# Every matmul of the mixture's up and down products is issued as two of 256 tokens with the same weights

## The reference

```python
ctx = causal_ema(x, tau_ctx)
wg = sigmoid([x, ctx] @ Wg.T + bg); gated = x * wg
h1 = gelu(x @ Wn1.T + bn1); mod = 0.5 + sigmoid(h1 @ Wn2.T + bn2)
traces = [causal_ema(gated * mod[d], tau[d]) for d in range(8)]
temporal = sum(traces * softmax(blend))
gate = sigmoid(temporal @ Wtemp.T + btemp); soma = gelu(x @ Wsoma.T + bsoma)
x = x + layernorm((soma * gate) @ Wout.T) * gamma + beta
```

```python
s0, s1, s2 = [relu(x @ share_wi[i]) @ share_wo[i] for i in range(3)]
expert_out = wa * relu(x @ expert_wi[t]) @ expert_wo[t] + wb * relu(x @ expert_wi[t + 1]) @ expert_wo[t + 1]
g = softmax(relu([expert_out[:, 0], s0[:, 0], s1[:, 0], s2[:, 0]] @ gate_w1) @ gate_w2)
x = x + g[0] * expert_out + g[1] * s0 + g[2] * s1 + g[3] * s2
```

## Time and profile before

| | |
|---|---|
| time, median of 3 runs | 1166.73 us (1166.54 to 1167.99) |
| the profiled execution's own time | 1168.23 us |
| its span, first to last instruction | 1166.2 us |
| mean granted clock of PE | 0.969 |
| PE, PEld busy | 1093.4, 869.8 us |
| DVE, ACT, POOL busy | 798.5, 410.6, 121.0 us |

### The profile page before, as it was taken

The page is one execution under the profiler, slowest core; times in us unless marked ns, Lnnn a source line. Parts: engine busy times, 40 slices in busy tenths (PEclk is TensorE's granted clock), DMA queues, the critical chain, the costliest instruction groups (busy, mean ns, idle before and its releaser), DMA issues.

```text
span 1166.2 us, 12367 instructions
## 1 busy us (share of the span) xinstructions
PE 1093.4 (94%) x4706; PEld 869.8 (75%) x4706; DVE 798.5 (68%) x1223; ACT 410.6 (35%) x638; POOL 121.0 (10%) x50
## 2 busy tenths in 40 slices
PE   7699677989889999999999999999999999999998
PEld 5177456768678887888878887788878888788886
DVE  7975996638965589465975589465975589545225
ACT  7155333643224422343233422343233422332221
POOL 2814445512000000000000000000000000000000
PEclk9599988989999999999999999999999999999999
DMA  5058794478835546354645456354644465455550
GB/s 213 5 198 291 282 347 150 179 285 279 311 136 194 181 181 234 112 201 181 230 144 198 180 182 219 124 198 173 243 145 164 176 218 201 144 180 199 206 179 30
DMA packets 37772, 224.30 MB, mean 192 GB/s; under 512 B 4498, under 2 KB 4754, under 8 KB 16082
## 3 DMA queue, kind: packets, MB, share of 16 engines
q1 hardware_dynamic: 37714, 223.52, 53.2%
HBM read 189.82 MB, written 33.69 MB: 192 GB/s over the span
## 4 chain that ended last, share of the span: by engine, by line
PE 59%; DVE 33%; DMA 3%; issue 2%; ACT 2%; SPq 0%; DVEq 0%; ACTq 0%
PE ps_down L590 8%; PE ps_up L590 8%; PE ps_down L592 8%; PE ps_up L592 8%; PE ps_up L591 8%; PE ps_down L591 8%; DVE trace L1168 6%; DVE temporal L1183 5%; DVE hid_lo L1068 5%; DVE trace L1176 5%; DVE trace L1171 5%; PE ps_aux L590 3%; PE ps_aux L591 3%; PE ps_aux L592 3%; DMA split_wi<-ex 2%
## 5 line engine op out<-in xcount | busy, mean ns | idle before, releaser
L1068 DVE SCALAR_TENSOR_TENSOR hid_lo<-ps_up,hid_hi 128x512 fp32r<-128x512 f32 x320 | 219.5, 687 | 330.8 <-ACT hid_hi L864 329.5
L864 ACT ACTIVATE hid_hi<-ps_up 128x512 fp32r<-128x512 f32 x320 | 191.6, 599 | 495.7 <-PE ps_up L592 495.4
L590 PE MATMUL ps_down<-hid_hi,wo 128*128 128x512 f32 x640 | 257.7, 403 | 40.4 <-ACT y L876 22.7
L590 PE MATMUL ps_up<-x_hi,wi 128*128 128x512 f32 (+1 forms) x644 | 257.1, 399 | 3.0 <-DMA wi<-split_wi 2.9
L592 PE MATMUL ps_down<-hid_hi,wo 128*128 128x512 f32 x640 | 254.5, 398 | 0.0
L592 PE MATMUL ps_up<-x_hi,wi 128*128 128x512 f32 (+1 forms) x644 | 253.2, 393 | 0.0
L591 PE MATMUL ps_up<-x_lo,wi 128*128 128x512 f32 (+1 forms) x644 | 253.2, 393 | 0.0
L591 PE MATMUL ps_down<-hid_lo,wo 128*128 128x512 f32 x640 | 251.4, 393 | 0.0
L590 PEld LDWEIGHTS ps_down<-hid_hi,wo 128*128 128x128 f32 x640 | 120.9, 189 | 74.2 <-issue 30.0
L590 PEld LDWEIGHTS ps_up<-x_hi,wi 128*128 128x128 f32 x644 | 121.5, 189 | 30.5 <-DMA wi<-split_wi 3.8
L592 PEld LDWEIGHTS ps_down<-hid_hi,wo 128*128 128x128 f32 x640 | 121.2, 189 | 29.8
(11 more groups left out here) (197 smaller groups left out, 1004.3 us busy)
## 6 DMA issues: line engine op xcount, KB each, us to landing
wi<-split_wi SPq DMA_DIRECT2D x70, 1024.0 KB, 4.9
wo<-split_wo SPq DMA_DIRECT2D x70, 1024.0 KB, 4.8
modb<-mod_scratch SPq DMA_DIRECT2D x28, 512.0 KB, 4.5
split_wi<-ex SPq DMA_DIRECT2D x8, 1024.0 KB, 8.7
split_wo<-ex SPq DMA_DIRECT2D x8, 1024.0 KB, 9.3
split_wi<-wi SPq DMA_DIRECT2D x6, 1024.0 KB, 7.5
split_wo<-wo SPq DMA_DIRECT2D x6, 1024.0 KB, 8.3
xt<-in_x SPq DMA_DIRECT2D x8, 512.0 KB, 3.6
```

The source lines that it names most:

```text
L590: pe.matmul(ps, w_hi, x_hi, start=start, stop=False)
L864: act.activation(hid_hi[:, k % NU, :], ps_up[k % NU][:, :], ACT.Relu).then_inc(hid_hi_ready, 1)
L1068: dve.scalar_tensor_tensor(hid_lo[:, k % NU, :], ps_up[k % NU][:, :], 0.0, f32(hid_hi[:, k % NU, :]), ALU.max, ALU.subtract).then_inc(hid_ ...
```

## The change

`up` (for all 512 tokens) and `down` call a new function `halves` in place of `product`. It makes each of the three matmuls as two, of tokens 0 to 255 and 256 to 511, with the same weights, one behind the other, into the two halves of the same PSUM bank. The flag that starts an accumulation is set on the first of the six matmuls alone, the one that ends it on the last alone. The opening's two `up` tiles, which were in halves already, keep `product`, as do all steps of the first block.

```diff
+            def halves(ps, w_hi, w_lo, x_hi, x_lo, start, stop):
+
+                for i, (w, x) in enumerate(((w_hi, x_hi), (w_hi, x_lo), (w_lo, x_hi))):
+                    for h in range(2):
+                        mm = pe.matmul(ps[:, half(h)], w, x[:, half(h)], start=start and i == 0 and h == 0, stop=stop and i == 2 and h == 1)
+                return mm
+
             def up(b, k, parity, tokens=slice(0, T), done=True):
...
-                    mm = product(ps, wi_hi[:, u % 2, at], wi_lo[:, u % 2, at], x2_hi[:, parity, c, tokens],
-                                 x2_lo[:, parity, c, tokens], c == 0, c == CT - 1)
+                    parts = halves if tokens == slice(0, T) else product
+                    mm = parts(ps, wi_hi[:, u % 2, at], wi_lo[:, u % 2, at], x2_hi[:, parity, c, tokens],
+                               x2_lo[:, parity, c, tokens], c == 0, c == CT - 1)
...
-                    mm = product(ps_down[c][:, :], wo_hi[:, u % 2, at], wo_lo[:, u % 2, at], hid_hi[:, k % NU, :],
-                                 hid_lo[:, k % NU, :], k % TPF == 0, k % TPF == TPF - 1)
+                    mm = halves(ps_down[c], wo_hi[:, u % 2, at], wo_lo[:, u % 2, at], hid_hi[:, k % NU, :],
+                                hid_lo[:, k % NU, :], k % TPF == 0, k % TPF == TPF - 1)
```

## The result

| | before | after |
|---|---|---|
| time, median of 4 runs each on one chip | 1167.14 us (1166.54 to 1167.99) | 1178.09 us (1177.81 to 1181.44) |
| the profiled execution's own time, span | 1168.23, 1166.2 us | 1178.31, 1176.3 us |
| mean granted clock of PE | 0.969 | 0.978 |

A forecast was written before the change was run, and what follows sets the result against it. PE was taken to set the time except where DVE is full in each period. Profiled 1168.23 us − 7.4 from shorter products + 1.5 for a clock fall = 1162.3, against the median 1160.8; predicted 1161 us, range 1157 to 1171.

The forecast's parts named there:

- Two of 256. The trace has them: Mixture products on PE: two halves at 113.8 ns make 227.6 ns, 3.3 ns less than one matmul of 512.
- The upper bound of 117.8: Slower `out` run at 201.45 us, POOL beside it: 117.8 ns a half, a pair 235.6 ns, 4.7 more than 512.
- What a load costs: PE's weight loads, listed at 189 ns, overlap in the run of `out`; a load's duration is not its price.
- C: Rival: loads can't overlap in a long stream, 378 ns a product, 563 us more, 1730 us; chance 0.01.
- The 2230 matmuls: Products of 512 counted where PE sets the time, 278 in each period; at 3.3 ns each, 7.4 us saved.
- 660: Products counted after the last stall, 16 slots and the last period less two ups: 192 + 468.
- The 180 before 330 us: Products counted at PE's pace before 330 us: 117 from 82.0 to 109.1 us, some 60 estimated by eye.
- Stalls and clock: PE's stalls behind ScalarE's copy to y grow from 3.0 to 3.7 us; one more clock fall costs 1.5 us.
- Instruction supply: PE's instruction queue: some 30 more packets, fetched while PE works, cost nothing; upper bound 0.9 us.
- Rival A: Nothing measurable: a half costs about 115.4 ns in a long stream, or DVE's stretch reaches further; 1166.0 us, chance 0.14.
- D: Rival: the second load of the same weights is dropped, 213.5 ns a product, 39 us saved, 1128 us; chance 0.03.
- B: Rival: in a long stream beside other engines' work a half costs more than half; 4.7 ns a product, 1177 us; chance 0.20.

The follow-up runs named there:

- e4_w64: The changed kernel with 64 of 128 weight columns in all but the first and last term of an accumulation; 1167.83 us, one execution.
- e6_uneven: The changed kernel with each matmul split into 384 and 128 tokens in place of 256 and 256; 1330.0 us, one execution.
- e11_later_halves: The changed kernel with the first block's steps from the rounding of temporal on one slot later; 1170.84 us, ratio 1.0021.
- e5_w64_512: The kernel before, 512 token columns a matmul, with 64-column weights in the middle of each accumulation; 1166.46 us, one execution.
- e8_later: The kernel before with the first block's steps from ScalarE's rounding of temporal on one slot later on every engine; 1147.24 us, ratio 0.9816.
- e1: The changed kernel with halves in the up products alone, down as before the change; 1173.96 us, ratio 1.0048.
- e2: The changed kernel with halves in the down products alone, up as before the change; 1172.0 us, ratio 1.0024.
- e3: The changed kernel with the three matmuls of tokens 0 to 255 first, then the three of 256 to 511; 1180.39 us, ratio 1.0103.
- e9: The changed kernel with 96 of 128 weight columns in all but the first and last term of an accumulation; 1163.48 us, one execution.
- e10_320: The changed kernel with each matmul split into 320 and 192 tokens in place of 256 and 256; 1227.09 us, one execution.
- e7_quarters: Each matmul made as four of 128 tokens with the same weights, in place of the changed kernel's two of 256; 1923.18 us, one execution.

## Why the prediction was wrong, step by step

- **"Two of 256. The trace has them" is the step that failed**: the term 113.8 ns a half was mis-sized, and with it the sign. It was read from runs of 24 halves; a stream of them costs 119.1, so that two are 238.2 and not 227.6 ns, 7.3 more than one of 512 instead of 3.3 less. The upper bound of 117.8 was real, but I put it down to POOL's work. A half costs the same beside a full DVE and an almost idle one.
- **What a load costs** was the wrong question as put. I asked whether 189 ns of load can overlap, found that they do, and took the price for nothing. The price of a load and matmul of 128 is 111.6 ns: nothing under 512 columns, and one half of a tie under 256. By the Trainium skill, section Performance Expectations of its page Trainium Kernel Development and Optimization, the busy share of the loads is a good metric of how near a kernel is to its limit. It went from 75 to 90% for 1% of time, so it told of the right resource and not of the price: C's 1730 us was far off.
- **The 2230 matmuls** held only for the tail (4.9 us, 4.8 by its 660). A period has 342 at PE's pace for 278, because DVE's `temporal` did not end when it did before but 2.5 us later. The 180 before 330 us are not borne out: that part is 2.2 us shorter, from a cause that stays open. A fall costs 1.6 to 1.7 us, near the 1.5 taken.
- **Stalls and clock** went the other way, as they must with the sign of a half: I said 3.7 us and one more fall. Five of the six went from 3.0 to 1.5 us from start to start, the first stayed at about 3, and four falls became one.
- **Instruction supply** at nothing was right: 67 packets, and still one wait for "issue", of 1.1 us.
- **Rival A's** 115.4 ns in a long stream is exceeded. **D** is refuted by 8534 loads. **B** had the direction, through "what a load and a matmul cost beside their columns", but a product became 7.3 ns longer where it said 4.7. That its 1177 us is within 1 us of the median is luck: it left out the falls that came back. Its condition, other engines at work, isn't what decides. The fixed 2.5 ns for each matmul that stood beside it, from the Trainium skill, TensorE: Matmul & The Clock Gate, section "Wait — 56ns, not 53.3ns?", had the right sign, but not the size: a product became 7.3 ns longer, and the quarters cost what their loads do, not what their columns do.

Shown by runs: a half costs 119.1 ns in a stream of them, order, number of instructions and other engines' work don't set that price, and shorter loads (with smaller outputs) lower it. Fitted by the splits with whole outputs, but not shown as a mechanism: that each step takes the longer of load and columns. Not tested: short loads under 128 token columns, so that the 111.6 ns could also be the least that a load and its matmul take together, whatever the load's length. Open: how the last 6 ns arise where the two are nearly equal. The last section has a sign that they depend on the stream, and not on load and columns alone.

## What to carry to other kernels

In this kernel a matmul of 128 weight columns hides its load only if its token columns take clearly longer than 112 ns; at 256 the two tie, and each of the four splits that keep the columns and add loads cost time. Price a form that will run a thousand times in a row by a long run of it, and if the trace has only short ones that disagree (113.8 and 117.8 here), take the disagreement as the size of what isn't known. A slower PE can hide in its own stalls, so test such a change also where the stalls are gone: the move that removed them was worth 1.8%, the change 2.1% there and 1.0% here.

## What the runs showed of the hardware that I hadn't expected

Short runs of halves have two rhythms, 113.5 and 118 ns. The opening's halves, the same instructions in every kernel of this study that has them, begin in the kernel after like this:

```profile
80.66 0.28 PE L590 MATMUL ps_up<-x_hi,wi 128*128 128x256 f32 x1
...
83.03 0.39 PE L598 MATMUL ps_up<-x_hi,wi 128*128 128x256 f32 x2
...
84.39 0.40 PE L598 MATMUL ps_down<-hid_hi,wo 128*128 128x256 f32 x2
```

and in the kernel with loads of 64 columns like this:

```profile
80.75 0.28 PE L591 MATMUL ps_up<-x_lo,wi 128*128 128x256 f32 x1
...
83.46 0.40 PE L599 MATMUL ps_up<-x_hi,wi 128*128 128x256 f32 x2
```

The first are 113.0 ns apart (33 starts in 3.73 us, the first 12 of the mixture's own halves among them), the second 117.8 (23 in 2.71). From 84.39 us on, the kernel after never again runs at 113 for long: down halves at 120, up halves at 118. Counting before and after, the opening ran at 113.5 in ten kernels and at 118 in three: `e4_w64`, `e6_uneven` and `e11_later_halves`. The 24 halves of `out`, which no version changes, tell more. Their first start and that of the next matmul are these in the kernel after, and then in the one with loads of 64 columns:

```profile
746.13 0.28 PE L590 MATMUL ps_aux<-wc_hi,xg_hi 128*128 128x256 f32 x1
...
748.96 0.40 PE L598 MATMUL ps_up<-x_hi,wi 128*128 128x256 f32 x2
...
744.11 0.28 PE L590 MATMUL ps_aux<-wc_hi,xg_hi 128*128 128x256 f32 x1
...
746.83 0.39 PE L599 MATMUL ps_up<-x_hi,wi 128*128 128x256 f32 x2
```

That is 117.9 ns a half in the kernel after (2.83 us), where the earlier trace rows had 113.8, and 113.3 ns among short loads (2.72 us), with the whole loads of 128 columns in all three. Behind 340 us each kernel has six such runs, and they agree within a nanosecond: 113.3 to 114.2 ns in the three kernels with 512s (before, `e5_w64_512`, `e8_later`), 117.8 in six with halves (after, `e1`, `e2`, `e3`, `e9`, `e11`), 113.3 in `e4_w64`, 115.3 in `e10_320`, 116.5 in `e7_quarters` and 120.0 in `e6_uneven`. So the same 24 instructions cost more or less with the kernel around them, and the run that the prediction took its price from stood among 512s. What sets the rhythm I couldn't find; that load and columns tie at 256 isn't all of it.

And the clock falls more often at longer stalls here. Counted over PE's waits for the copy to `y` in eight kernels from 325 us on (before, after, `e1` to `e5` and `e9`): 21 falls at 26 stalls with PE idle for 2.5 us and more, 5 at 11 of 1.8 to 2.2 us, and none at 10 of 1.3 us.
